# Attention over gathered neighbour rows: who adds the node's own row, VectorE or the gather itself

## What is computed

```python
xc = x[row]; xn = x[col]
h = relu(xc @ W1[:d] + xn @ W1[d:] + b1)
mask = sigmoid(h @ W2 + b2)[:, 0]
w = mask / (segment_sum(mask, row)[row] + 1e-09)
agg = segment_sum(w[:, None] * xn, row)
```

## Time and profile before

| | |
|---|---|
| time before, median of 3 runs | 4972.48 us (4972.26 to 4973.69) |
| the profiled execution's own time | 4971.88 us |
| its span, first to last instruction | 4970.1 us |
| mean granted clock of PE | 0.912 |
| attention block, from POOL's first gather to its last indirect DMA | 619.30 to 1712.87 us |
| DMA queue that POOL fills, share of the 16 DMA engines' span | 29.3% |

### The profile page before, as it was taken

The page is one execution under the profiler, slowest core; times in us unless marked ns, Lnnn a source line. Parts: engine busy times, 40 slices in busy tenths (PEclk is TensorE's granted clock), DMA queues, the critical chain, the costliest instruction groups (busy, mean ns, idle before and its releaser), DMA issues. The chain is left out here.

```text
span 4970.1 us, 48372 instructions
## 1 busy us (share of the span) xinstructions
PE 3739.1 (75%) x16011; PEld 1589.9 (32%) x16011; DVE 3885.0 (78%) x5124; ACT 943.7 (19%) x2780; POOL 3103.7 (62%) x3043
## 2 busy tenths in 40 slices
PE   1801068766766399999976989798987898969897
PEld 0401022222222134444432434333433343424343
DVE  4698488877877567777757888798887988878887
ACT  0100010000000198888841000010001000010000
POOL 5200377777777534444435777777776777767777
PEclk9999579988888799999988999899998999989998
DMA  9995365544545399999965444444444444444443
GB/s 361 397 402 233 87 201 168 169 144 145 172 139 154 98 211 206 208 208 209 207 138 157 135 140 136 118 141 132 140 130 126 137 133 133 132 134 135 140 137 95
DMA packets 359755, 843.42 MB, mean 170 GB/s; under 512 B 97017, under 2 KB 174559, under 8 KB 359327
## 3 DMA queue, kind: packets, MB, share of 16 engines
q0 software_dynamic: 137488, 313.46, 29.3%
q1 hardware_dynamic: 172624, 436.91, 24.9%
q10 hardware_dynamic: 49392, 89.94, 5.7%
HBM read 597.79 MB, written 242.28 MB: 169 GB/s over the span
## 5 line engine op out<-in xcount | busy, mean ns | idle before, releaser
L2429 PE MATMUL c_wide<-c_choice,c_parts 128*128 128x512 fp8e4 x8232 | 1881.7, 387 | 283.1 <-DVE c_odd L2514 136.9
L2303 POOL DMA_INDIRECT c_ring<-table,near x1288 | 1293.6, 1004 | 445.7 <-issue 327.9
L2429 PEld LDWEIGHTS c_wide<-c_choice,c_parts 128*128 128x128 bf16 x8232 | 797.8, 99 | 1337.2 <-DVE c_odd L2514 195.8
L2514 DVE TENSOR_TENSOR c_odd<-c_odd,c_wide 128x1024 f32<-128x1024 f32 x644 | 783.5, 1217 | 55.5 <-PE c_wide L2429 52.7
L2514 DVE TENSOR_TENSOR c_even<-c_even,c_wide 128x1024 f32<-128x1024 f32 x672 | 817.5, 1217 | 8.1 <-PE c_wide L2429 1.9
L1529 PE MATMUL a_wide<-a_choice,a_parts 128*128 128x512 fp8e4 x2058 | 526.6, 402 | 181.9 <-DVE a_hidden L1612 168.8
L1924 ACT ACTIVATE b_mass<-b_onehot,mask_r 128x128 f32<-128x128 bf16 x2058 | 607.2, 387 | 100.2 <-DVE b_onehot L2004 73.9
L1983 PE MATMUL b_agg<-b_mass,b_h_row 128*128 128x512 f32 (+1 forms) x1372 | 561.0, 558 | 74.1 <-DMA b_mass<-masks 74.0
L1894 POOL DMA_DIRECT2D b_mass<-masks x343 | 299.6, 962 | 475.5 <-ACT b_mass L1924 359.7
L1612 DVE TENSOR_TENSOR a_hidden<-a_wide,a_minus_bt 128x1024 f32<-128x1024 f32 x343 | 417.1, 1216 | 132.4 <-PE a_wide L1529 132.1
L1414 POOL DMA_INDIRECT masks<-a_value,a_cell x379 | 428.1, 1130 | 115.5 <-issue 114.6
(11 more groups left out here) (352 smaller groups left out, 2992.5 us busy)
## 6 DMA issues: line engine op xcount, KB each, us to landing
c_choice<-chosen SPq DMA_DIRECT2D x196, 896.0 KB
masks<-n_zeros SPq DMA_DIRECT2D x196, 784.0 KB, 8.0
b_mass<-masks POOLq DMA_DIRECT2D x343, 448.0 KB, 11.6
a_pick_row<-picks ACTq DMA_DIRECT2D x343, 256.0 KB
chosen<-a_choice SPq DMA_DIRECT2D x49, 896.0 KB, 5.4
c_ring<-table,near POOLq DMA_INDIRECT x1288
c_source<-table SPq DMA_DIRECT2D x28, 448.0 KB, 6.0
c_own_rows<-own_xh SPq DMA_DIRECT2D x14, 448.0 KB, 6.0
```

The costliest lines, as they stand in the source:

```text
L2303: pool.indirect_dma_start(ring[:, at + j, :], None, table1[layer % 2], bass.IndirectOffsetOnAxis(of_u[:, j:j + 1], 0)).then_inc(landed[n % ...
L2429: last = pe.matmul(wide[q][:, lo_c:hi_c], parts[:, s, part, :], choice[e][:, s % CHUNK, lo_c:hi_c], start=(part == 0), stop=(part == 2))
L2514: dve.tensor_tensor(side[:, :], side[:, :], found, ALU.max).then_inc(taken, 1)
```

## The change

The tiles whose ring places were used before (`LAID`, 45 of 49 tiles, 340 of the 379 lists; all but 0, 1, 2 and 5) are done in another way. As soon as the places are free, ACT copies the tile's own row into each of them (`lay_own`, 45 copies) and raises `own_laid`. POOL's gathers of these tiles wait for that and are issued with `compute_op=ALU.add`, so that the DMA adds the table's rows to what lies in the ring. DVE does the first of the three operations only for tiles 0, 1, 2 and 5. `LAID_AFTER[u]` is the number of weighed tiles after which tile u is laid: that of `A_PLACES`, made to never fall from one tile to the next, since ACT works in order. A copy stands on ACT right behind the sigmoid of the last of those tiles. The arithmetic is otherwise the same.

```diff
--- before.py
+++ after.py
@@ -1252,6 +1252,8 @@
         A_PLACES, A_LANDED = ring_places(CAP, TILES, A_RING, A_FLOWS), landed_counts(CAP, TILES, A_FLOWS)
         WEIGHED_AT = tuple(max(A_FIRST, reduced_at(CAP, u, A_LAG)) for u in range(TILES))
         VALUED_AT = tuple(at + 3 if at + 3 < SELECTS else AT_END for at in WEIGHED_AT)
+        LAID = tuple(u for u in range(TILES) if A_PLACES[u][1] > 0)
+        LAID_AFTER = {u: max(A_PLACES[v][1] for v in LAID if v <= u) for u in LAID}
         TURN_AT = (5, 10)
         COLS, A_HIDDEN = 4, 5
         WIDEST = max(CAP)
@@ -1322,6 +1324,7 @@
             masks_copied = sem("a_masks_copied")
             landed = [sem(f"a_landed{f}") for f in range(A_FLOWS)]
             rows_did = sem("a_rows_did")
+            own_laid = sem("a_own_laid")
             cells_did = sem("a_cells_did")
             logit_made = sem("a_logit_made")
             weight_made = sem("a_weight_made")
@@ -1396,16 +1399,21 @@
             @block.gpsimd
             def _(pool):
                 def gather_tile(u):
-                    at, after = A_PLACES[u]
-                    if after > 0:
-                        pool.wait_ge(logit_made, after)
+                    at = A_PLACES[u][0]
+                    if u in LAID:
+                        pool.wait_ge(own_laid, LAID.index(u) + 1)
                     for j in range(CAP[u]):
                         g = FIRST[u] + j
                         if g >= A_RING and g % 2 == 0 and allowed_at(CAP, g, A_EARLY) > 0:
                             pool.wait_ge(taken, allowed_at(CAP, g, A_EARLY))
-                        pool.indirect_dma_start(ring[:, at + j, :], None, table_a,
-                                                bass.IndirectOffsetOnAxis(list_of(u)[:, j:j + 1], 0)
-                                                ).then_inc(landed[u % A_FLOWS], 16)
+                        if u in LAID:
+                            pool.indirect_dma_start(ring[:, at + j, :], None, table_a,
+                                                    bass.IndirectOffsetOnAxis(list_of(u)[:, j:j + 1], 0),
+                                                    compute_op=ALU.add).then_inc(landed[u % A_FLOWS], 16)
+                        else:
+                            pool.indirect_dma_start(ring[:, at + j, :], None, table_a,
+                                                    bass.IndirectOffsetOnAxis(list_of(u)[:, j:j + 1], 0)
+                                                    ).then_inc(landed[u % A_FLOWS], 16)
 
                 def store_tile(u):
                     pool.wait_ge(value_made, u + 1)
@@ -1474,6 +1482,12 @@
                     act.wait_ge(logit_made, u + 1)
                     act.activation(value[:, mine], value[:, mine], ACT.Sigmoid, bias=b2[:, :]
                                    ).then_inc(weight_made, 1)
+
+                def lay_own(u):
+                    at = A_PLACES[u][0]
+                    act.wait_ge(logit_made, LAID_AFTER[u])
+                    act.wait_ge(own_loaded[u // RANGE], 16)
+                    act.copy(ring[:, at:at + CAP[u], :], bc(own_b[:, u:u + 1, :], [P, CAP[u], D])).then_inc(own_laid, 1)
 
                 for n in range(A_PICKS):
                     load_pick(n)
@@ -1496,9 +1510,15 @@
                     for u in range(TILES):
                         if n == WEIGHED_AT[u] + 1:
                             weigh_tile(u)
+                            for later in LAID:
+                                if LAID_AFTER[later] == u + 1:
+                                    lay_own(later)
                 for u in range(TILES):
                     if WEIGHED_AT[u] + 1 >= SELECTS:
                         weigh_tile(u)
+                        for later in LAID:
+                            if LAID_AFTER[later] == u + 1:
+                                lay_own(later)
                 make_masks(RANGES - 1)
                 bodies = bodies_of(act)
                 with act.Fori(0, bodies) as j:
@@ -1675,10 +1695,10 @@
                     at, size = A_PLACES[u][0], CAP[u]
                     full, mine = [P, size, D], ring[:, at:at + size, :]
                     dve.wait_ge(landed[u % A_FLOWS], A_LANDED[u])
-                    if u % RANGE == 0:
+                    if u not in LAID:
                         dve.wait_ge(own_loaded[u // RANGE], 16)
-                    rows.did(dve.tensor_tensor(mine, mine, bc(own_b[:, u:u + 1, :], full), ALU.add))
-                    rows.wait()
+                        rows.did(dve.tensor_tensor(mine, mine, bc(own_b[:, u:u + 1, :], full), ALU.add))
+                        rows.wait()
                     rows.did(dve.scalar_tensor_tensor(mine, mine, 0.0, bc(w2_row[:, :].unsqueeze(1), full),
                                                       ALU.max, ALU.mult))
                     rows.wait()
```

## The result

The changed kernel takes 5143.16 us (median of 4 runs, 5139.17 to 5149.57) against 4972.37 us before (4 runs). The ratio is 1.0346, 95% interval 1.0328 to 1.0364: 171 us slower. The forecast was 5161 us, 18 us more.

What follows compares the result with a forecast made beforehand. POOL was taken to bound the attention block: 210 us for accumulating gathers, less 16 for the port and 5 for the waits, gives +189 on 4972.5, about 5161 us; range 5085 to 5280.

Steps and rivals of the forecast that it cites:

- POOL as the bound: Attention block: POOL is occupied for practically all of its 1067.5 us; DVE with PE is second by some 60 us.
- The price of an accumulating gather: POOL's 340 accumulating gathers: 0.618 us more each, 210 us in all, carried over from the accumulating scatter.
- my lower bound of 0.603: Extra us per accumulating gather on POOL, by the scatter's minima: times 340, 205 us.
- rival B: POOL's gathers: add costs less into SBUF than HBM, up to 0.5 us; 5056 to 5121 us; chance 0.09.
- rival C: POOL's accumulating gathers of 512-byte rows cost more than the scatter's: 5223 us at 0.8 extra, 5291 at 1.0; chance 0.12.
- rival A: POOL's gathers: the add is free with destination in SBUF; -21 us, 4951 us; chance 0.12.
- the upper bound: POOL's 340 accumulating gathers: longest accumulating scatter against shortest plain gather, 0.711 us more each, 242 us.
- The rule of the Trainium skill on two read descriptors: POOL's gathers: three descriptors in place of two if time went by descriptors, 1.44 us each, 163 us in all.
- The port between DVE and POOL: POOL DMAs that start during DVE's two-SBUF-input adds are stretched; dropping 45 adds gives 16 us back, bounds 0 and 38.
- Copies and their wait: ACT's 45 copies, about 48 us, are hidden in its idle time; POOL's wait for them has slack: cost 0.
- The waits for `taken`: POOL's 5 us of real waiting for DVE vanish as POOL reaches tiles 4 and 5 later: -5 us.
- DVE's wait for landings: DVE in the attention block: its wait for gathered rows rises from 59 to about 300 us.

Runs made afterwards that it cites:

- experiment 2: The kernel before without the 45 DVE adds, nothing in their place: 4961.82 us, ratio 0.9971.
- experiment 8: The kernel before with the attention block's 343 comparisons moved from DVE to ACT: 4898.52 us, ratio 0.9850.
- experiment 1: The changed kernel with plain gathers in place of accumulating ones, ACT's copies and POOL's waits kept: 4962.43 us, ratio 0.9979.
- experiments 5 to 7: Fewer rows per gather: 64 plain (changed kernel without the gathers' add), 4934.63 us; 64 and 96 accumulating (changed kernel), 5103.88 and 5104.55 us.
- experiment 5: The changed kernel with plain gathers, copies and waits kept, and 64 rows per gather in place of 128: 4934.63 us.
- experiment 3: The changed kernel with ACT laying zeros instead of own rows and DVE adding own rows for all 49 tiles: 5152.18 us, ratio 1.0355.

## Why the prediction was right

The forecast was near, and for the reasons given: POOL bounds the block, and the add's price comes on top of each gather. **POOL as the bound** held. The changed kernel's block grew by 171.9 us and POOL's groups account for 172.0 of it, and relief of DVE of 53 us (experiment 2) or 228 us (experiment 8) showed only as far as POOL's own DMAs got shorter.

**The price of an accumulating gather** was the term that decided, and it was carried over from another transfer, the accumulating scatter to HBM: 0.618 us by medians, 0.594 measured, so 202 us instead of 210, below my lower bound of 0.603 by little. The 8 us too many come from the partner: I took the gather's 958 ns from the scatter's 1576, where the plain scatter's own median gives 1576 - 986 = 0.590 us, 201 us in all; by minima 0.603 for the scatter stands beside 0.596 for the gather. That a destination in SBUF is much cheaper (rival B, 0.5 us at most) is not so, rival C's 0.8 to 1.0 us is not so either, and rival A, the free add, is refuted by experiment 1 against the changed kernel. My reason for carrying it over was half wrong. I argued that POOL's time goes by rows, since 512 and 4 bytes cost the same. They nearly do, 940 and 954 ns, but experiments 5 to 7 show that it hardly goes by rows either, at least from 64 to 128: it goes by DMAs. That the wrong reason did no harm is luck, as both had 128 rows. The 242 us of the upper bound had left out the 5 us for `taken`; it should have been 237.

**The rule of the Trainium skill on two read descriptors** ("Collectives: The Full Stack", the bandwidth ceiling) would have given 1.44 us as an estimate; 1.55 was measured. The transfer itself does look different: the page counts 175568 packets in POOL's DMA queue for the changed kernel and 137488 with plain gathers (experiment 1), 112 more for each of 340 gathers, with the same megabytes.

```profile
q0 software_dynamic: 175568, 313.46, 30.0%
```

```profile
q0 software_dynamic: 137488, 313.46, 29.8%
```

But POOL's price is not proportional to that. With 96 rows the queue has 164688 packets, 80 more per gather, and with 64 rows 153808, 48 more; with plain gathers it has 137488 at 64 rows (experiment 5) as at 128. From 112 down to 48 packets more, the price goes only from 0.596 to 0.514 us. The statement of the Trainium skill that rival A drew on ("Collectives: The Full Stack", Stop 4, where the add happens), that the compute engines are free, is made of collectives. Carried over to a DMA that POOL issues itself it fails in this trace: POOL pays 0.6 us more for issuing it.

**The port between DVE and POOL.** For the adds I had 16 us (bounds 0 and 38). The medians of experiments 1 and 2 say 11 and 12, POOL's groups 10.3 in experiment 2 and 11.6 in experiment 3, but only 6.6 in experiment 1: so 7 to 12. That DVE's additions stretch POOL's DMAs is shown by this; that a shared port is the cause is not tested by any run.

The whole relief in the changed kernel is larger. Before, the groups were 831.5 us busy; with 340 x 0.594 = 202 more it would be 1033.5; it was 1008.4, so 25 us less. About 12 are the adds. The other 13 also appear in experiment 3, which has all adds (1020.0), so they come with the longer DMAs. Experiment 1 and the changed kernel, which differ in the add of the DMAs alone, say the same: 1008.4 - 824.9 = 183.5 us instead of 202, so 18 less. The prediction has no term for it. Part of it is that with fewer DMAs in a given time fewer start while DVE compares, 183 by my count instead of 275. But each of these loses more, 0.25 us over the shortest of its kind instead of 0.20, so that all of them lose 46 us instead of 54. That explains 8 us; the other 5 to 10 are open.

**Copies and their wait** cost 0, as said: 43.3 us on an idle ACT (48 estimated), 0.3 us of waiting, experiments 1 and 2 equal within 1 us. **The waits for `taken`** went from some 5 us to nothing: gaps -4.9.

The sum was 210 - 16 - 5 = 189; measured 202 - 25 - 5 = 172. DVE's wait for landings rose to 268 us, not 300: the block grew by 17 us less than forecast, and DVE waits 12 us more for PE (143.9 instead of 132.1). The errors are in the sizes of two terms, 8 and 9 us, both to the same side, and in the second 13 to 18 of the 25 us are an effect that the prediction doesn't have, while the adds gave 7 to 12 of the 16. So that the whole came out within 18 us is in part luck.

## What to carry to other kernels

Find out first whether a queue of indirect DMAs is the bound: a busy share of 77% with a gap of 0.30 us before each DMA is full occupation, and then only the number and duration of its DMAs count. Moving arithmetic from a compute engine into such DMAs lengthens them on the issuing engine, and where that engine is the bound this decides, however idle the adding is elsewhere; here the break-even was at 0.06 us per gather and the price is 0.6. What shortens the bound may stand on another engine: here comparisons on DVE stretched POOL's DMAs by 72 us in all, and moving them to an idle engine was worth 1.5%.

## What the runs showed of the hardware

- An indirect DMA's time on POOL hardly depends on its rows from 64 to 128: 0.893 us for 64, 0.905 for 96, 0.940 for 128, and the fixed gap of 0.30 us comes on top. With an add 1.407, 1.433 and 1.536 us.
- It hardly depends on bytes per row together with the side that is indexed either (the two were not varied alone): an accumulating scatter of 4-byte elements to HBM takes 1.557 us at least, an accumulating gather of 512-byte rows to SBUF 1.536.
- A gather of 128 rows of 512 bytes makes 112 packets more when it adds, 80 more with 96 rows and 48 more with 64, with the same bytes.
- POOL's DMAs lose time to DVE's comparison (bf16 in, 8-bit float out, 0.79 us) and to DVE's additions of two SBUF operands: 72 us for 343 comparisons and 7 to 12 us for 45 additions. They hardly do to the take with one input in PSUM: 0.97 us on average for 323 DMAs that start within one (experiment 8).
